# Start of a two-layer decoder: weights of the quantised attention loaded and quantised ahead of the tokens

## The chip, the cores and the metric

One core of one Trainium2 chip. The metric is the device time of one execution in microseconds (us), the median of several runs of the whole program. The profile is one further execution taken by the hardware profiler.

## The reference, cut to what matters

The kernel computes two decoder layers on x of shape (32, 56, 256), float32, with a context of shape (32, 1500, 64). Each layer adds three parts to x in turn, each fed with a layer norm of x:

```python
x = x + quantised_attention(layernorm(x))          # layer 0, the stage of this case
x = x + latent_cross_attention(layernorm(x), ctx)
x = x + mixture_of_experts_16(layernorm(x))
x = x + rotary_attention(layernorm(x))             # layer 1
x = x + causal_cross_attention(layernorm(x), ctx)
x = x + mixture_of_experts_7(layernorm(x))
```

The quantised attention rounds its four weight matrices (256 x 256 each) to -1, 0 or 1 times a scale, the mean magnitude of the whole matrix:

```python
def act_quant(x):
    scale = 127.0 / clip(max(abs(x), axis=-1), EPS)
    return clip(round(x * scale), -128, 127) / scale
def bit_linear(x, W):
    s = clip(mean(abs(W)), EPS)
    return x @ (clip(round(W / s), -1, 1) * s).T
```

The rounding of the weights needs no token; the statistics of the layer norm need no weight. Both must be there before the first tile of tokens can be projected.

## The kernel before, in words

The tokens live in one tile `x_res`, 128 partitions x 16 tiles x 256 values. Two sequences of 56 tokens share a tile of 128 partitions: one on partitions 0 to 55, the other on 64 to 119. Partitions 56 to 63 and 120 to 127 hold no token and must hold zeros.

The program is a row of blocks. In a block every engine has its own list of instructions, and all engines meet at a block's end. The first three blocks are those of this case:

- **Setup** (`setup`, lines 115 to 162). SyncE (SP) loads the identity and a head mask (L143, L144). GpSimd (POOL) writes zeros over all of `x_res` (L153) and then over a tile `zero` (L154). SP waits for the first of these, issues the two loads of the tokens (L148), and waits until all has landed (L149). VectorE (DVE) writes zeros over the eight banks (L158) and converts the identity (L161).
- **Statistics** (`row_stats`, lines 189 to 259). SP loads the quantised stage's weights, 1 MB, with one transfer (L996). Beside this DVE makes the layer norm's statistics: 16 instructions over the 16 tiles of tokens in a loop (L223), 16 that combine them (L228), a copy and an addition (L230, L231), then ScalarE's (ACT) root (L254) and DVE's reciprocal (L234). POOL writes zeros to buffers of the next block. Every later stage calls `row_stats` too.
- **The quantised attention's own block** (`self_attention`, from line 1041). SP waits for the weights, prefetches the six weight tensors of the latent stage (L1939), and then issues three long transfers of zeros to scratch memory that the experts' stages will use (`clear_scratch`, L170, L173). DVE makes a small mask (L1415), then quantises the weights (L1426 to L1459): it sums magnitudes (L1429, L1432), TensorE (PE) adds them over the partitions with one product (L1254), DVE makes scales (L1436, L1438), and each of four matrices is scaled and rounded (L1441, L1442, L1446 or L1450). Then come the 16 tiles of tokens, software-pipelined over all engines; the first instruction of the first tile is the normalisation (L1616).

The order within an engine is the order of the text, written out by hand; a semaphore's wait stops everything behind it on its engine. All the transfers named here are issued by SP and go through its one hardware queue.

Of the kernel before, what the change touches and what calls it, by code (L numbers as in the profile page):

```python
# [7 lines left out]
ALU = mybir.AluOpType  # L8
# [5 lines left out]
AX_X = mybir.AxisListType.X  # L14

P = 128
B, T, D = 32, 56, 256
# [30 lines left out]
def ds(start, size):  # L48
    return bass.ds(start, size)
# [65 lines left out]
def setup(nc, ctx, t):  # L115

    k = {"sems": [], "used": [], "held": ExitStack(), "past": ExitStack()}

    def sb(name, shape, dt=F32):
        return ctx.enter_context(nc.sbuf_tensor(name, shape, dt))  # L120

    k["x"] = sb("x_res", [P, NT, D])
    k["id32"] = sb("id32", [P, P])
    k["id16"] = sb("id16", [P, P], F16)
    k["hmask"] = sb("hmask", [P, 8])
    k["ps"] = ctx.enter_context(nc.psum_tensor("banks", [P, 8, 512], F32))
    k["xg"] = [nc.dram_tensor(f"sent_rows_{layer}", (block_count(layer) * BN + 512, ROW), F16,
                              kind="Internal").ap() for layer in range(2)]
    k["ytok"] = nc.dram_tensor("sent_outputs", (2 * NT * P + block_count(0) * BN, D), F32,
                               kind="Internal").ap()  # L130
    k["zero"] = sb("zero", [P, ROW])
    k["rows_sent"] = [ctx.enter_context(nc.semaphore(f"rows_sent_{c}")) for c in range(2)]
    k["y_sent"] = [ctx.enter_context(nc.semaphore(f"y_sent_{s}")) for s in range(3)]
    k["zeroed"], k["nzero"] = ctx.enter_context(nc.semaphore("scratch_zeroed")), 48
    loaded = ctx.enter_context(nc.semaphore("setup_loaded"))
    loaded_id = ctx.enter_context(nc.semaphore("setup_identity_loaded"))
    zeroed = ctx.enter_context(nc.semaphore("setup_zeroed"))
    x, id32, id16 = k["x"], k["id32"], k["id16"]
    src = t["x"].rearrange("(t two) q d -> two q t d", two=2)
    with nc.Block() as block:  # L140
        @block.sync
        def _(sp):
            sp.dma_start(id32[:], t["ident"]).then_inc(loaded_id, 16)  # L143
            sp.dma_start(k["hmask"][:], t["hmask"]).then_inc(loaded, 16)  # L144

            sp.wait_ge(zeroed, 1)
            for two in range(2):
                sp.dma_start(x[two * HALF:two * HALF + T, :, :], src[two]).then_inc(loaded, 16)  # L148
            sp.wait_ge(loaded, 48)  # L149

        @block.gpsimd
        def _(pool):
            nc.gpsimd.memset(x[:], 0.0).then_inc(zeroed, 1)  # L153
            nc.gpsimd.memset(k["zero"][:], 0.0).then_inc(zeroed, 1)  # L154

        @block.vector
        def _(dve):
            nc.vector.memset(k["ps"][:], 0.0)  # L158

            dve.wait_ge(loaded_id, 16)  # L160
            nc.vector.tensor_copy(id16[:], id32[:])  # L161
    return k


# [21 lines left out]
            sp.wait_ge(stored, 32)  # L186


def row_stats(nc, ctx, name, k, double=False, load=None, zero=None):

# [10 lines left out]
    var_made = new_sem(nc, k, f"{name}_var_made")  # L203
    rooted = new_sem(nc, k, f"{name}_rooted")
    x = k["x"]
    with nc.Block() as block:
        if load:
            block.sync(load)

        @block.gpsimd  # L210
        def _(pool):
# [4 lines left out]
        @block.vector  # L216
        def _(dve):
            s = Steps(dve, own)

            with dve.Fori(0, NT // 8) as n:  # L220
                for u in range(8):
                    i = n * 8 + u
                    nc.vector.bn_stats(  # L223
                        raw[:, ds(i, 1), :].rearrange("p o d -> p (o d)"),
                        x[:, ds(i, 1), :].rearrange("p o d -> p (o d)")).then_inc(own_bn, 1)
            dve.wait_ge(own_bn, NT)
            for i in range(NT):
                s(nc.vector.bn_aggr(mv[:, i, :], raw[:, i, :]))  # L228
            s.settle()
            s(nc.vector.tensor_copy(st["mean"][:], mv[:, :, 0]))  # L230
            nc.vector.tensor_scalar(var[:], mv[:, :, 1], HEPS, None, ALU.add).then_inc(var_made, 1)  # L231

            dve.wait_ge(rooted, 1)
            s(nc.vector.reciprocal(st["r"][:], sd[:, 0, :]))  # L234
            if double:
                s.settle()
                s(nc.vector.tensor_tensor(var[:], mv[:, :, 1], st["r"][:], ALU.mult))
                s.settle()
                s(nc.vector.tensor_tensor(sd[:, 2, :], var[:], st["r"][:], ALU.mult))
                s.settle()  # L240
                s(nc.vector.tensor_scalar(var[:], sd[:, 2, :], HEPS, None, ALU.add))
                s.settle()
                nc.vector.tensor_scalar(sd[:, 0, :], sd[:, 2, :], float(D) / 4, None,
                                        ALU.mult).then_inc(var_made, 1)

                dve.wait_ge(rooted, 3)
                s(nc.vector.reciprocal(sd[:, 2, :], sd[:, 1, :]))
                s.settle()
                s(nc.vector.tensor_tensor(st["rt"][:], st["r"][:], sd[:, 2, :], ALU.mult))
# [637 lines left out]
def self_attention(nc, k, t, kind, prefetch=None):  # L887
# [9 lines left out]
    with ExitStack() as ctx:  # L897
# [3 lines left out]
        def sem(name):  # L901
            return new_sem(nc, k, f"{kind}_{name}")
# [50 lines left out]
        if bit:  # L953
# [8 lines left out]
            ones, one = sb("ones", [P, P]), sb("one", [P, 1])  # L962
            E2, magic = sb("E2", [P, H, T]), sb("magic", [P, 2])
            wsum_done, asum_made, vq_made = sem("weight_sums_done"), sem("asum_made"), sem("vq_made")
            yo_made, x_added, e2_made = sem("outputs_made"), sem("outputs_added"), sem("scaled_exp_made")
        elif rot:
            NW = 768
# [68 lines left out]
                nc.gpsimd.memset(magic[:, 0:1], MAGIC).then_inc(own_pool, 1)  # L1036
                nc.gpsimd.memset(magic[:, 1:2], -MAGIC).then_inc(own_pool, 1)

        st = row_stats(nc, ctx, f"{kind}_stats", k, double=rot, load=load_weights, zero=zero_buffers)

        with nc.Block() as block:
            @block.sync
# [203 lines left out]
            def _(pe):  # L1246
# [1 line left out]
                pe.wait_ge(loaded, NLOAD)  # L1248
                rounds = 2 if bit else 4
                hp = H // rounds  # L1250
                if bit:

                    pe.wait_ge(asum_made, 1)
                    nc.tensor.matmul(Y[:, 0:4], ones[:], asum[:], start=True,  # L1254
                                     stop=True).then_inc(wsum_done, 1)
                if not rot:
                    pe.wait_ge(dve_prepared, 1)

# [147 lines left out]
            def _(dve):  # L1406
                s = Steps(dve, own)

                def then(ins):

                    s(ins)
                    s.settle()
# [9 lines left out]
                        hgm[:], m4[:].unsqueeze(2).broadcast_to([P, 4, 2]),  # L1422
                        hgb[:].unsqueeze(1).broadcast_to([P, 4, 2]), ALU.mult))
                dve.sem_inc(m4_made, 1)
                if bit:
                    s(nc.vector.memset(ones[:], 1.0))  # L1426
                    for m in range(4):
                        for c in range(2):
                            s(nc.vector.tensor_reduce(dq[:, 2 * m + c:2 * m + c + 1], wraw[:, c, m, :],  # L1429
                                                      AX_X, ALU.add, apply_absolute_value=True))  # L1430
                    s.settle()
                    nc.vector.tensor_reduce(asum[:], dq[:, 0:8].rearrange("p (m c) -> p m c", c=2),  # L1432
                                            AX_X, ALU.add).then_inc(asum_made, 1)

                    dve.wait_ge(wsum_done, 1)
                    then(nc.vector.tensor_scalar(sw[:], Y[:, 0:4], 1.0 / (D * D), QEPS, ALU.mult,  # L1436
                                                 ALU.max))
                    then(nc.vector.reciprocal(rsw[:], sw[:]))  # L1438
                    for m in range(4):
                        wm = wraw[:, :, m, :]  # L1440
                        then(nc.vector.tensor_scalar(wm, wm, rsw[:, m:m + 1], MAGIC, ALU.mult, ALU.add))  # L1441
                        then(nc.vector.tensor_scalar(wm, wm, MAGIC, 1.0, ALU.subtract, ALU.min))  # L1442
                        dst = wq[:, :, m * D:(m + 1) * D] if m < 3 else wo[:]
                        if m < 2:
                            for c in range(2):
                                then(nc.vector.tensor_scalar(  # L1446
                                    dst[:, c].rearrange("p (q a e) -> p q a e", a=2, q=2),
                                    in_halves(wm[:, c]), -1.0, None, ALU.max))
                        else:
                            then(nc.vector.tensor_scalar(dst, wm, -1.0, None, ALU.max))  # L1450
                        if m < 3:
                            then(nc.vector.tensor_copy(
                                swrow[:, 16 * m:16 * m + 16], sw[:, m:m + 1].broadcast_to([P, 16])))
                if causal:
                    then(nc.vector.tensor_copy(idb[:], id32[:]))
                    nc.vector.tensor_copy(cmask[:], cmask32[:].unsqueeze(1).broadcast_to([P, 8, T])
                                          ).then_inc(dve_prepared, 1)
                if bit:
                    nc.vector.tensor_copy(ax[:, 1:2], sw[:, 3:4]).then_inc(dve_prepared, 1)  # L1459
                if not rot:  # L1460
                    dve.wait_ge(dve_prepared, 1)
                dve.wait_ge(prepared, 2)
# [1829 lines left out]
```

## Time and profile before

| | us |
|---|---|
| median of 3 runs | 2020.77 |
| lowest, highest | 2019.04, 2022.14 |
| the profiled execution's own time | 2014.04 |
| its span, first to last instruction | 2012.3 |
| VectorE busy over the span | 1466.8 (73%) |
| TensorE busy over the span | 1526.3 (76%) |

In a line of the timeline the first number is the start in us from the start of the span, the second the busy time; then engine, source line, operation, what it writes and reads, and in brackets the idle time ahead of it with what ended it. `SPq` is SP issuing a transfer: the time there is that of the issue, not of the transfer. `PEq L140` as releaser is the meeting of all engines at a block's end.

### The profile page before, as it was taken

How to read it: one execution, taken by the hardware profiler on the slowest of the kernel's cores; microseconds unless marked ns; L12 is line 12 of the kernel's file. 1: busy time of each engine (PE TensorE's matmuls, PEld its weight loads, DVE VectorE, ACT ScalarE, POOL GpSimd, SP SyncE). 2: the span in 40 equal slices, each digit the busy share in tenths (PEclk: the TensorE clock that was granted, in tenths of full speed). 3: DMA queues.
4: the chain of work that ended last, by engine and by line, in shares of the span. 5: the costliest groups of instructions: out<-in, count | busy, mean ns of one | idle time of the engine just before them, and what ended most of it. 6: DMA issues, size and time to landing. Idle time of an engine off the chain costs nothing. (4 is left out here: it accounts for less than half of the span.)

```text
span 2012.3 us, 37357 instructions
## 1 busy us (share of the span) xinstructions
PE 1526.3 (76%) x12412; PEld 927.7 (46%) x12412; DVE 1466.8 (73%) x2589; ACT 1010.4 (50%) x1630; POOL 643.5 (32%) x636
## 2 busy tenths in 40 slices
PE   0555558799999999999996755953777659956992
PEld 0333336443333333333333745942556436644792
DVE  6989872479999999999996784445766635576674
ACT  0555451376666666666663243532544535544461
POOL 1111100124545454554530144642343200026241
PEclk9756555599999999999997857976788879967996
DMA  7910000011111111111110124551000010023334
GB/s 205 301 40 0 0 0 16 16 26 46 39 48 36 50 34 50 34 50 39 45 26 2 30 87 141 174 165 30 1 1 0 0 24 1 0 78 118 92 110 146
DMA packets 78562, 115.88 MB, mean 58 GB/s; under 512 B 12369, under 2 KB 59401, under 8 KB 78051
## 3 DMA queue, kind: packets, MB, share of 16 engines
q1 hardware_dynamic: 70691, 93.35, 16.8%
q0 software_dynamic: 7776, 21.28, 3.0%
q8 instruction: 58, 0.95, 0.2%
q14 instruction: 37, 0.30, 0.1%
HBM read 59.73 MB, written 40.19 MB: 50 GB/s over the span
## 5 line engine op out<-in xcount | busy, mean ns | idle before, releaser
L2408 DVE TENSOR_TENSOR lat_dsum<-lat_dsum,lat_Pb 125x896 f32<-125x896 f32 x320 | 416.7, 1302 | 58.6 <-ACT lat_Pb L2342 52.1
L2342 ACT ACTIVATE lat_Pb<-banks 125x896 f32<-125x896 f32 x384 | 331.5, 915 | 173.2 <-PE banks L2265 171.9
L2220 PE MATMUL banks<-lat_Pb,lat_kv 125*64 125x448 f32 x1536 | 331.0, 552 | 0.0
L2259 PE MATMUL banks<-lat_QH,lat_kT 128*125 128x448 f16 x768 | 183.7, 361 | 2.9 <-DVE lat_QT L2366 1.9
L2175 POOL TENSOR_TENSOR lat_kk<-lat_rot,lat_kk 125x768 f16<-125x768 f32 x32 | 71.2, 2225 | 315.4 <-ACT lat_kk L2314 315.4
L2220 PEld LDWEIGHTS banks<-lat_Pb,lat_kv 125*64 125x64 f32 x1536 | 93.1, 136 | 153.3 <-issue 152.6
L2259 PEld LDWEIGHTS banks<-lat_QH,lat_kT 128*125 128x125 f16 x768 | 89.4, 136 | 114.1 <-ACT lat_Pb L2342 89.9
L2707 POOL DMA_INDIRECT sent_outputs<-moe_yb,moe_yidx x98 | 94.9, 968 | 120.0 <-ACT moe_yb L2948 104.8
L2843 PE MATMUL banks<-moe_w2d,moe_gT 88*128 (+3 forms) x780 | 103.1, 283 | 17.6 <-DVE moe_gT L3127 14.0
L2265 PE MATMUL banks<-lat_QL,lat_kT 64*125 64x448 f16 x768 | 113.7, 375 | 0.0
L2161 POOL TENSOR_TENSOR lat_rot<-lat_raw,lat_cosK 125x768 f32<-125x768 f32 x32 | 73.7, 2303 | 92.7 <-DMA lat_raw<-in_ctx_dram 88.1
L2381 DVE RECIPROCAL lat_rD<-banks 128x448 f32<-128x448 f32 x32 | 94.3, 2946 | 1.9 <-PE banks L2231 1.9
L2843 PEld LDWEIGHTS banks<-moe_w2d,moe_gT 88*128 88x128 f16 (+1 forms) x780 | 76.4, 101 | 33.2 <-issue 22.6
L2699 POOL DMA_INDIRECT sent_rows<-moe_arena,moe_idx x64 | 72.5, 1133 | 50.5 <-DVE moe_idx L3065 31.4
L3115 DVE COPY moe_xTb<-banks 128x1024 f16<-128x1024 f16 x49 | 33.9, 691 | 65.4 <-PE banks L2810 65.4
L2761 PE MATMUL banks<-moe_xTb,moe_w2i 128*88 128x256 f16 (+1 forms) x588 | 73.4, 275 | 0.0
L2305 ACT ACTIVATE lat_kT<-banks 128x1000 f16<-128x1000 f16 x64 | 51.1, 798 | 31.9 <-PE banks L2207 31.8
L2265 PEld LDWEIGHTS banks<-lat_QL,lat_kT 64*125 64x125 f16 x768 | 36.6, 131 | 63.6 <-issue 63.6
L2761 PEld LDWEIGHTS banks<-moe_xTb,moe_w2i 128*88 (+1 forms) x588 | 62.6, 112 | 4.2 <-issue 1.0
L1123 POOL TENSOR_TENSOR x_res<-x_res,bit_yo 128x256 f32 (+1 forms) x16 | 11.6, 727 | 162.1 <-DVE bit_yo L1495 162.1
L2169 POOL TENSOR_TENSOR lat_rot<-lat_rot 125x768 f32<-125x768 f32 x32 | 58.7, 1834 | 2.5
L427 POOL TENSOR_TENSOR rot_rt<-rot_y,rot_msin 128x256 f32<-128x256 f32 x32 | 34.4, 1074 | 68.8 <-DVE rot_msin L777 67.5
(421 smaller groups left out, 3331.1 us busy)
## 6 DMA issues: line engine op xcount, KB each, us to landing
moe_xb<-sent_rows SPq DMA_DIRECT2D x49, 257.0 KB, 2.9
lat_raw<-in_ctx_dram SPq DMA_DIRECT2D x32, 375.0 KB
moe_arena<-sent_outputs SPq DMA_DIRECT2D x16, 512.0 KB, 7.6
sent_rows<-zero SPq DMA_DIRECT2D x1, 7453.0 KB, 51.3
lat_QH<-lat_QT SPq DMA_DIRECT2D x64, 112.0 KB, 2.2
lat_QL<-lat_QT SPq DMA_DIRECT2D x64, 112.0 KB, 2.2
sent_rows<-zero SPq DMA_DIRECT2D x1, 5140.0 KB, 68.5
sent_outputs<-zero SPq DMA_DIRECT2D x1, 4096.0 KB, 40.9
```

The source lines that it names most:

```text
L2161: s(nc.gpsimd.tensor_tensor(rot[:, par], r, cosK[:], ALU.mult))
L2175: nc.gpsimd.tensor_tensor(halves(par, True), paired(rot[:, par]), halves(par, False), ALU.subtract).then_inc(kl_made, 1)
L2220: ins = nc.tensor.matmul(ps[u * DC:(u + 1) * DC, 4 + par, 0:8 * T], kv[:, par, tt, :], Pb[:, tt % NPB, u, :], start=tt == 0, stop=tt == KT ...
L2259: nc.tensor.matmul(ps[0:KP, 2 * u + tt % 2, 0:8 * T], kT[:, par, tt, 0:KP], queries(QH, u), start=True, stop=False)
L2265: ins = nc.tensor.matmul(ps[0:KP, 2 * u + tt % 2, 0:8 * T], kT[rows, par, tt, 0:KP], queries(QL, u, rows), start=False, stop=True)
L2342: nc.scalar.activation(Pb[:, slot:slot + 2, u, :], ps[0:KP, 2 * u:2 * u + 2, 0:8 * T], ACT.Exp, scale=1.0 / QSCALE).then_inc(exp_done, 1)
L2381: s(nc.vector.reciprocal(rD[:], ps[:, 7, 0:8 * T]))
L2408: ins = nc.vector.tensor_tensor(dsum[:, par], dsum[:, par], Pb[:, tt % NPB], ALU.add)
L2699: nc.gpsimd.indirect_dma_start(xg[:, :], bass.IndirectOffsetOnAxis(ap=idx[:, c, i:i + 1], axis=0), rows[:, i, :], None).then_inc((sent0, s ...
L2707: nc.gpsimd.indirect_dma_start(ytok[:, :], bass.IndirectOffsetOnAxis(ap=yidx[:, n, h:h + 1], axis=0), yb[:, n % 3, h, :], None).then_inc(y ...
L2761: ins = nc.tensor.matmul(ps[0:FP, dst, j * BN:(j + 1) * BN], w[:, u, c, j * FP:(j + 1) * FP], rhs(v, c), start=a + c == 0, stop=a == 2 and ...
L2843: ins = nc.tensor.matmul(dst, gT2[:, n % 2, u, j, h * P:(h + 1) * P], w[:, v, j, :], start=a + j == 0, stop=last and not (gated and b < 0))
```

## The change

- Setup keeps the identity, the mask and the `zero` tile. The writing of zeros over `x_res` and the loads of the tokens leave it.
- The loads of the tokens become a function `load_x`, issued by SP in the statistics block behind the load of the weights. The tokens come in two parts of eight tiles. Each part has four transfers: two for the token rows and two that copy zeros from the `zero` tile to the eight unused partitions of each half. Each part has a semaphore of its own.
- DVE's quantisation of the weights, word for word as it was, and PE's product for the sums move from the attention's block to the head of the statistics block. DVE then waits for the first part of the tokens, makes eight statistics, waits for the second part and makes eight more. In this call the loop over the tiles is written out.
- In the attention's block the small mask (L1415) stays where it is.

```diff
@@ setup
+    x_in = [ctx.enter_context(nc.semaphore(f"x_loaded_{part}")) for part in range(2)]
...
-            sp.wait_ge(zeroed, 1)
-            for two in range(2):
-                sp.dma_start(x[two * HALF:two * HALF + T, :, :], src[two]).then_inc(loaded, 16)
-            sp.wait_ge(loaded, 48)
+            sp.wait_ge(loaded, 16)
...
-            nc.gpsimd.memset(x[:], 0.0).then_inc(zeroed, 1)
             nc.gpsimd.memset(k["zero"][:], 0.0).then_inc(zeroed, 1)
...
+    def load_x(sp):
+        sp.wait_ge(zeroed, 1)
+        for part in range(2):
+            tiles = slice(part * NT // 2, (part + 1) * NT // 2)
+            for two in range(2):
+                r = two * HALF
+                sp.dma_start(x[r:r + T, tiles, :], src[two, :, tiles, :]).then_inc(x_in[part], 16)
+                sp.dma_start(x[r + T:r + HALF, tiles, :], k["zero"][0:HALF - T, 0:D].unsqueeze(1)
+                             .broadcast_to([HALF - T, NT // 2, D])).then_inc(x_in[part], 16)
+
+    k["load_x"], k["x_in"] = load_x, x_in
@@ row_stats
+    load_x = k.pop("load_x", None)
     with nc.Block() as block:
-        if load:
-            block.sync(load)
+        @block.sync
+        def _(sp):
+            if load:
+                load(sp)
+            if load_x:
+                load_x(sp)
+
+        if sums:
+            block.tensor(sums)
...
         @block.vector
         def _(dve):
             s = Steps(dve, own)
-
-            with dve.Fori(0, NT // 8) as n:
+            if ready:
+                ready(dve)
+
+            def eight(n):
                 for u in range(8):
...
+            if load_x:
+                for part in range(2):
+                    dve.wait_ge(k["x_in"][part], 64)
+                    eight(part)
+            else:
+                with dve.Fori(0, NT // 8) as n:
+                    eight(n)
@@ self_attention
+            own_weights = sem("dve_weights")
...
+        def quantised_weights(dve):
+            s = Steps(dve, own_weights)
...
+            dve.wait_ge(loaded, NLOAD)
+            s(nc.vector.memset(ones[:], 1.0))
...
+            nc.vector.tensor_copy(ax[:, 1:2], sw[:, 3:4]).then_inc(dve_prepared, 1)
+
+        def weight_sums(pe):
+            pe.wait_ge(asum_made, 1)
+            nc.tensor.matmul(Y[:, 0:4], ones[:], asum[:], start=True, stop=True).then_inc(wsum_done, 1)
+
+        st = row_stats(nc, ctx, f"{kind}_stats", k, double=rot, load=load_weights, zero=zero_buffers,
+                       ready=quantised_weights if bit else None, sums=weight_sums if bit else None)
...
-                if bit:
-
-                    pe.wait_ge(asum_made, 1)
-                    nc.tensor.matmul(Y[:, 0:4], ones[:], asum[:], start=True,
-                                     stop=True).then_inc(wsum_done, 1)
...
-                if bit:
-                    s(nc.vector.memset(ones[:], 1.0))
...
-                if bit:
-                    nc.vector.tensor_copy(ax[:, 1:2], sw[:, 3:4]).then_inc(dve_prepared, 1)
```

The lines left out in the last part are the body of the quantisation, the same in the old place and the new.

## Rows read from the trace of the kernel before

**Rows 1.** Timeline, VectorE alone, from the start to the first normalisation.

```profile
1.75 3.47 DVE L158 MEMSET banks<- 128x4096 f32 x1 [1.75 <-PEq L3282]
5.13 0.21 DVE L161 CAST id<-id 128x128 f16<-128x128 f32 x1
17.53 5.32 DVE L223 BATCH_NORM_STATS2 bit_stats_raw<-x_res  x16 [12.19 <-PEq L140]
...
24.62 0.25 DVE L234 RECIPROCAL bit_stats_r<-bit_stats_sd 128x16 f32<-128x16 f32 x1 [0.28 <-ACT bit_stats_sd L254]
25.20 0.16 DVE L1415 TENSOR_TENSOR bit_m<-hmask 128x4 f32<-128x4 f32 x1 [0.33 <-PEq L206]
25.57 0.17 DVE L1426 MEMSET bit_ones<- 128x128 f32 x1 [0.20 <-DVE bit_m L1415]
...
36.44 0.15 DVE L1459 COPY bit_ax<-bit_sw 128x1 f32<-128x1 f32 x1
36.63 0.41 DVE L1616 TENSOR_SCALAR bit_xtmp<-x_res,bit_stats_mean,bit_stats_r 128x256 f32<-128x256 f32 x1
```

**Rows 2.** Timeline, SyncE's issues, to the last transfer of zeros.

```profile
0.81 0.43 SPq L143 DMA_DIRECT2D id<-in_ident_dram  x1
1.30 0.41 SPq L144 DMA_DIRECT2D hmask<-in_hmask_dram  x1
4.35 0.92 SPq L148 DMA_DIRECT2D x_res<-in_x_dram  x2
17.18 0.41 SPq L996 DMA_DIRECT2D bit_wraw<-in_bit_w_dram  x1
25.14 0.56 SPq L1939 DMA_DIRECT2D lat_wqr<-in_lat_wqr_dram  x1
...
28.45 38.14 SPq L170 DMA_DIRECT2D sent_rows<-zero  x2
66.64 18.43 SPq L173 DMA_DIRECT2D sent_outputs<-zero  x1
```

**Rows 3.** Waits of SyncE: who waited for whom, total us, times, longest us.

```profile
SPq L140 <- DMA x_res<-in_x_dram: 11.5, 1, 11.5
```

**Rows 4.** Windows at the start: us, busy by engine, granted clock, DMA share, GB/s.

```profile
4.00:6.00 2.00, 0.00 (x0) 0.00 (x0) 1.34 (x2) 0.00 (x0) 0.79 (x2) 1.00 0.13 36
...
14.00:16.00 2.00, 0.00 (x0) 0.00 (x0) 0.00 (x0) 0.00 (x0) 0.00 (x0) 1.00 0.72 123
...
18.00:19.00 1.00, 0.00 (x0) 0.00 (x0) 1.00 (x4) 0.47 (x1) 1.00 (x2) 1.00 0.73 78
...
21.00:22.00 1.00, 0.00 (x0) 0.00 (x0) 1.00 (x4) 0.00 (x0) 0.00 (x0) 1.00 0.49 197
```

**Rows 5.** Transfers issued before 70 us: KB each, us from issue to landing.

```profile
sent_outputs<-zero SPq DMA_DIRECT2D x1, 4096.0 KB, 40.9
lat_wq<-in_lat_wq_dram SPq DMA_DIRECT2D x1, 2048.0 KB, 18.2
...
x_res<-in_x_dram SPq DMA_DIRECT2D x2, 896.0 KB
...
bit_wraw<-in_bit_w_dram SPq DMA_DIRECT2D x1, 1024.0 KB, 4.9
lat_wqr<-in_lat_wqr_dram SPq DMA_DIRECT2D x1, 768.0 KB, 6.4
...
id<-in_ident_dram SPq DMA_DIRECT2D x1, 64.0 KB, 1.9
```

**Rows 6.** Windows over three tiles each of the quantised stage, columns as in rows 4.

```profile
59.86:109.40 49.54, 27.38 (x212) 17.68 (x216) 44.30 (x116) 27.12 (x43) 5.32 (x8) 0.69 0.98 288
109.40:158.50 49.10, 27.20 (x191) 16.78 (x184) 44.43 (x116) 24.20 (x39) 6.03 (x9) 0.53 0.00 0
```

**Rows 7.** First users of what SyncE sends ahead: timeline of TensorE, tile `sent_rows`.

```profile
314.13 1.51 PE L1983 MATMUL banks<-lat_wkr,lat_wqr 64*96 64x64 f32 x8 [3.53 <-PEq L1041]
...
L2699 POOL DMA_INDIRECT sent_rows<-moe_arena,moe_idx x64: 956/962/5527, 1187.9 to 1867.3; - x64
```

More of the change, by code:

```diff
@@ L186, in _, with row_stats @@
             sp.wait_ge(stored, 32)
-def row_stats(nc, ctx, name, k, double=False, load=None, zero=None):
+def row_stats(nc, ctx, name, k, double=False, load=None, zero=None, ready=None, sums=None):
     def sb(n, shape):
@@ L1037, in zero_buffers, with then @@
                 nc.gpsimd.memset(magic[:, 1:2], -MAGIC).then_inc(own_pool, 1)
-        st = row_stats(nc, ctx, f"{kind}_stats", k, double=rot, load=load_weights, zero=zero_buffers)
+        def quantised_weights(dve):
+            s = Steps(dve, own_weights)
+            def then(ins):
+                s(ins)
+                s.settle()
+            dve.wait_ge(loaded, NLOAD)
+            s(nc.vector.memset(ones[:], 1.0))
+            for m in range(4):
+                for c in range(2):
+                    s(nc.vector.tensor_reduce(dq[:, 2 * m + c:2 * m + c + 1], wraw[:, c, m, :],
+                                              AX_X, ALU.add, apply_absolute_value=True))
+            s.settle()
+            nc.vector.tensor_reduce(asum[:], dq[:, 0:8].rearrange("p (m c) -> p m c", c=2),
+                                    AX_X, ALU.add).then_inc(asum_made, 1)
+            dve.wait_ge(wsum_done, 1)
+            then(nc.vector.tensor_scalar(sw[:], Y[:, 0:4], 1.0 / (D * D), QEPS, ALU.mult,
+                                         ALU.max))
+            then(nc.vector.reciprocal(rsw[:], sw[:]))
+            for m in range(4):
+                wm = wraw[:, :, m, :]
+                then(nc.vector.tensor_scalar(wm, wm, rsw[:, m:m + 1], MAGIC, ALU.mult, ALU.add))
+                then(nc.vector.tensor_scalar(wm, wm, MAGIC, 1.0, ALU.subtract, ALU.min))
+                dst = wq[:, :, m * D:(m + 1) * D] if m < 3 else wo[:]
+                if m < 2:
+                    for c in range(2):
+                        then(nc.vector.tensor_scalar(
+                            dst[:, c].rearrange("p (q a e) -> p q a e", a=2, q=2),
+                            in_halves(wm[:, c]), -1.0, None, ALU.max))
+                else:
+                    then(nc.vector.tensor_scalar(dst, wm, -1.0, None, ALU.max))
+                if m < 3:
+                    then(nc.vector.tensor_copy(
+                        swrow[:, 16 * m:16 * m + 16], sw[:, m:m + 1].broadcast_to([P, 16])))
+            nc.vector.tensor_copy(ax[:, 1:2], sw[:, 3:4]).then_inc(dve_prepared, 1)
@@ L1424, in _ @@
                 dve.sem_inc(m4_made, 1)
-                if bit:
-                    s(nc.vector.memset(ones[:], 1.0))
[L1427 to L1453, printed above, removed]
                 if causal:
```

## The prediction

> **What bounds the kernel now.** The change touches only the first 37 us of 2012, so I read that stretch and not the average shares. First VectorE's timeline [rows 1]: it finishes the setup at 5.34 (5.13 plus 0.21), stands idle for 12.19 us, makes statistics from 17.53, and from 25.57 to 36.59 (36.44 plus 0.15) quantises weights. At 36.63 the first tile of tokens is normalised. Between 17.53 and 36.63 VectorE hardly stops. So the start is one chain: tokens land, statistics, weights, first tile. Then SyncE's issues and waits [rows 2, 3]: the tokens are issued at 4.35 and SyncE waits 11.5 us for them, which is what VectorE's idle time is made of. The weights are issued only at 17.18, since the block of the tokens must end first; they are on the way while VectorE makes statistics. The last thing to see is that the two inputs differ in what they cost. The weights, 1024 KB, land 4.9 us after their issue [rows 5]. The tokens, 2 x 896 KB, keep the DMA busy from about 5.7 (it is busy for 0.13 of the window 4 to 6) to about 15.4 (0.72 of the window 14 to 16), and SyncE sees the end at about 16.8 [rows 3, 4]. The quick transfer is started last, behind the slow one. After the start VectorE is what the 16 tiles go by: it is busy for 44.3 of 49.5 us over three of them [rows 6].
>
> **The setup block** loses SyncE's long wait. What is left on each engine: VectorE until 5.34 [rows 1]; SyncE the identity, landed 1.9 us after its issue at 0.81, and the head mask, issued at 1.30 and far smaller [rows 2, 5]. No row gives the mask's landing; by the identity's it is at 3.2, so VectorE covers it. The zeros over the token tile are gone from GpSimd, but they too lay beside VectorE's work, so their removal by itself is worth nothing: they only held the tokens' issue, until 4.35. A block's end costs about 0.27 us: VectorE's last result before the next one is at 24.87, SyncE's next issue at 25.14 [rows 1, 2]. So the weights are issued at 5.34 + 0.27 = 5.61 in place of 17.18.
>
> **The weights land** at 5.61 + 4.9 = 10.5. That is their own row, with nothing queued behind them. Now eight transfers are queued behind. The first of the latent stage's loads, 768 KB with five more behind, took 6.4 [rows 5]; that gives 12.0 as the late end. Below 4.9 there is nothing to expect. I take 4.9, the same transfer, and keep the 1.5 us for the range.
>
> **VectorE's chain** is then: quantisation 36.59 - 25.57 = 11.0 us, PE's product and its wait included, giving 21.6. The statistics from their first instruction to the next block's first, 25.20 - 17.53 = 7.67 us, giving 29.25. The small mask with its wait, 25.57 - 25.20 = 0.37. The first normalisation starts at 29.6 against 36.63: **7.0 us less**. All of it is the 17.53 - 10.5 by which the chain starts sooner. No instruction of VectorE goes away, so the gain is idle time alone. The written-out loop and the waits are equal to the row within 0.3 us either way (VectorE starts 0.35 us after SyncE behind the meeting at 17.18, part of it the loop's set-up) [rows 1, 2]. TensorE and ScalarE have nothing else in that block; GpSimd's fills, 3 us, lie beside the wait for the weights.
>
> **Are the tokens there in time?** They are needed at 21.6 (first part) and, after eight statistics of 5.32 / 16 us each, at 24.3 (second part). SyncE issues nine transfers from 5.61, at about 0.45 each done by 9.8 [rows 2]: not a limit. In the queue's order the tokens follow the weights, whose bytes stopped moving at about 21.5 with an issue at 17.18 (0.49 of the window 21 to 22) [rows 2, 4]. In the new time base that is 10.0. The tokens' bytes take 15.4 - 5.7 = 9.7 us, so to 19.7, and the receipt 16.8 - 15.4 = 1.4 more: 21.1. The first part is there by about 17, well before 21.6. To this come four transfers of zeros, 256 KB in pieces of 1 KB, which the profile of before doesn't show. At the least they cost nothing (they may fill in where the tokens leave DMA engines unused). Priced as tokens, byte for byte, they add 9.7 x 256 / 1792 = 1.4 us: 22.5, under 24.3. At the most, if what counts is the number of partitions written (8 a transfer against 56 at equal bytes for each partition), each takes as long as a token transfer of its part, 9.7 / 4, and the four add 9.7: 30.8, that is 6.5 us late. The pieces, the queue and the source row are nearest to the tokens' own row, so I take 1.4, and **the tokens cost nothing**, with 1.8 us to spare. If that cover goes, each us of lateness beyond 24.3 is paid in full by VectorE.
>
> The Trainium skill speaks against this slack ("SBUF — State Buffer", Door 1: The DMA port swizzle): bandwidth depends on how many of 16 ports the partitions reach, and eight adjacent partitions 56 to 63 reach two. With its 435 GB/s over 16 ports a transfer of 64 KB would take about 1.2 us, an estimate from that page. Four of them would then add 4.8 us in place of 1.4 and the second part would land at 25.9, 1.6 us late; the gain would be 5.4. The trace of before has no transfer to eight partitions, so it shows neither.
>
> **What is moved past what.** The prefetch of the latent weights and the zeros to scratch memory start when the statistics block ends, at about 29.2 in place of 25.14: 4 us later. Their first users are at 314 and 1188 [rows 7], and the last of these transfers, behind the latent loads in the queue, landed at 66.64 + 40.9 = 107.5 [rows 2, 5]; at 112 it still has some 195 us to spare before the first user. I cost this at nothing. They now run 11 us later relative to the tiles of tokens, but three tiles under full DMA load took 49.54 us and three without any 49.10 [rows 6], so shifting that load is worth under 0.1 us. VectorE has no other wait added.
>
> **Sum**: -7.0 from the chain, 0 from the tokens, 0 elsewhere. Against the profiled execution's own 2014.04 (1.7 above its span of 2012.3) this is 2007.0. The profiled run is 6.7 below the median of the runs, more than the gain itself; I apply the difference to the median: 2020.8 - 7.0 = **2013.8**. A measurement of this kernel tells about 0.2%, 4.0 us, from no change. The three runs lie 3.1 us apart.
>
> **Rivals.**
> 1. **The second part is somewhat late**, by 1 to 3 us. Its cover is 24.3 - 21.1 = 3.2, so the four transfers of zeros must add 4.2 to 6.2, 1.1 to 1.6 each; the bounds above are 0.35 and 2.4 each. Then 4.0 to 6.0 remain, 2014.8 to 2016.8. Weights that land at 12.0 give the same: 5.5. For it: no row prices a transfer to eight partitions, and this lies midway between the bounds. Against it: the byte-for-byte price leaves 1.8 us. 20%. (The port estimate above, 1.2 us each, falls at its near end.)
> 2. **The zeros are as slow as whole token transfers**: the second part lands at 30.8, then eight statistics (2.66) and the rest of the chain up to the mask's end, 25.57 - 22.85 = 2.7: normalisation at 36.2. The gain is 0.4, 2020.4, no change. The wait has only gone from one end of the chain to the other. 7%.
> 3. **The weights are held up by the tokens** in the same queue, so that both land together at 22.5. Then VectorE's chain of 19.1 us starts there: 22.5 + 19.1 = 41.6, slower by 5.0, 2025.8. It decides at the wait ahead of the quantisation, and the tie is a landing at 17.5. Against it: the latent loads landed in the order of issue, 6.4 for the first and 18.2 for a later one [rows 5]. 4%.
> 4. **The chain shortens but the time doesn't follow**: 7 us are gained at the start and given back by a later stage that meets other clock or DMA phases. Nothing in the stage waits for a fixed time, so I see no place for it; yet the run-to-run spread is near half of the gain. Result within 4 us of before. 9%, a third of it on the slow side by chance.
> 5. **The change doesn't do what it says**: the two parts would be needless, since VectorE comes to the tokens only at 21.6. That changes the use of the split and not the sum, and has no share of its own.
>
> **How the numbers follow.** My forecast has 60%, the rivals 20, 7, 4 and 9. Faster by over 0.2%: 57 of the 60 (the rest to noise), 16 of the 20, 2 of the others: 0.75. Slower: 4 and 2, 0.06. Same: the remaining 0.19. The range: below, 7.3 us plus 2.5 of drift gives 2011. Above, it takes in the first rival and most of the noise: 2018.8.
>
> **What would show it.** VectorE's timeline of after should have: the first sum of magnitudes at 10.6, the first statistic at 21.6 with no wait, the ninth at 24.3 with no wait, the first normalisation at 29.6. The wait ahead of the quantisation should name the weights' transfer, landing 4.9 after an issue at 5.6. From the first normalisation on, all tiles should lie 7.0 us sooner, and the first product of the latent stage at 307 in place of 314. An idle time ahead of the ninth statistic proves the first or second rival, by its length; one ahead of the first sum beyond 10.6 the third. The prediction is wrong if the first normalisation is later than about 32.6.

## The result, and the profile after

The change makes the kernel faster by a third of a per cent: median 2012.56 us (17 runs) against 2019.04 us (17 runs of the kernel before), ratio 0.9965 with a 95% interval of 0.9951 to 0.9978. That is 7.1 us less by the ratio (2019.04 x 0.0035), 4.4 to 9.9 us by its interval, and 6.5 us by the medians. The forecast was 2013.8 us, 7.0 us less. The kernel before was measured anew beside the change, and its median over 17 runs lies 1.7 us under the 2020.77 on which the forecast was built.

VectorE's timeline of the kernel after, from the start to the first normalisation, answers to [rows 1]:

```profile
1.75 3.47 DVE L155 MEMSET banks<- 128x4096 f32 x1 [1.75 <-PEq L3318]
5.13 0.21 DVE L158 CAST id<-id 128x128 f16<-128x128 f32 x1
10.84 0.17 DVE L1076 MEMSET bit_ones<- 128x128 f32 x1 [5.50 <-DMA bit_wraw<-in_bit_w_dram]
10.92 2.64 DVE L1079 TENSOR_REDUCE bit_dq<-bit_wraw 128x1 f32<-128x256 f32 x8
...
21.64 0.15 DVE L1104 COPY bit_ax<-bit_sw 128x1 f32<-128x1 f32 x1
21.71 5.31 DVE L242 BATCH_NORM_STATS2 bit_stats_raw<-x_res 128x6 f32<-128x256 f32 x16
27.06 1.17 DVE L255 BATCH_NORM_AGGREGATE bit_stats_mv<-bit_stats_raw 128x2 f32<-128x6 f32 x16
...
29.37 0.16 DVE L1482 TENSOR_TENSOR bit_m<-hmask 128x4 f32<-128x4 f32 x1 [0.33 <-PEq L216]
29.76 0.41 DVE L1652 TENSOR_SCALAR bit_xtmp<-x_res,bit_stats_mean,bit_stats_r 128x256 f32<-128x256 f32 x1 [0.23 <-DVE bit_m L1482]
```

The idle time ahead of VectorE's first real work has shrunk from 12.19 us to 5.50, and what ends it is now the weights' transfer and no longer the end of the block with the tokens. Behind it the 16 statistics stand in one piece: 5.31 us without a gap, so neither wait for the tokens cost anything. The first normalisation starts at 29.76 in place of 36.63, 6.87 us sooner.

SyncE's issues in the kernel after answer to [rows 2]; the transfers' table gives size and time to landing, as in [rows 5]:

```profile
5.61 0.39 SPq L1024 DMA_DIRECT2D bit_wraw<-in_bit_w_dram  x1
6.04 0.50 SPq L166 DMA_DIRECT2D x_res<-in_x_dram  x1
6.59 0.89 SPq L167 DMA_DIRECT2D x_res<-zero  x1
...
10.37 0.53 SPq L166 DMA_DIRECT2D x_res<-in_x_dram  x1
10.94 2.10 SPq L167 DMA_DIRECT2D x_res<-zero  x1
29.32 0.57 SPq L1975 DMA_DIRECT2D lat_wqr<-in_lat_wqr_dram  x1
```

```profile
bit_wraw<-in_bit_w_dram SPq DMA_DIRECT2D x1, 1024.0 KB, 5.2
...
x_res<-zero SPq DMA_DIRECT2D x4, 64.0 KB
```

The weights are issued at 5.61 and land in 5.2 us. SyncE's nine issues last until 13.04 (10.94 plus 2.10), and not until 9.8 as forecast: those of the zeros take 0.71 to 2.10 us each. It costs nothing, since the DMA is never without work meanwhile: its share is 0.88 or more in every microsecond from 8 to 20. The 6.9 us arrive at the next stage undiminished; the timeline of TensorE, as in [rows 7]:

```profile
307.18 1.51 PE L2019 MATMUL banks<-lat_wkr,lat_wqr 64*96 64x64 f32 x8 [3.53 <-PEq L1113]
```

That is 6.95 us ahead of the 314.13 of before. At the end of the span the two profiles lie 5.7 us apart (2006.6 against 2012.3). Between, each stage adds or takes some tenths; the last section takes this scatter up.

### The profile page after: what moved, and what is told of

Its sections match the earlier page's. It is cut to its first block and busy times, and to the rows that moved or that the text cites. A ratio compares the mean times of both kernels' runs of the same rounds, so it can differ in the third digit from the quotient of the medians.

```text
span 2006.6 us, 37326 instructions
## 1 busy us (share of the span) xinstructions
PE 1526.6 (76%) x12412; PEld 928.0 (46%) x12412; DVE 1466.8 (73%) x2589; ACT 1010.3 (50%) x1630; POOL 642.7 (32%) x635
```

## The experiments

Each kernel is the kernel after with the edit shown, if nothing else is said. Each ratio is to runs of the kernel before taken beside it. "First normalisation" is the start of the first instruction of the first tile: 36.63 before, 29.76 after.

**The loads moved alone.** VectorE keeps the order of before.

```diff
             s = Steps(dve, own)
-            if ready:
-                ready(dve)
...
             s(nc.vector.reciprocal(st["r"][:], sd[:, 0, :]))
+            if ready:
+                ready(dve)
```

> The loads moved alone: weights and tokens issued in the statistics block as in the change, but VectorE makes the statistics first and quantises after them, as before. My theory: the gain needs the order as well. The second part of the tokens lands at about 21.9 (DMA quiet at 20.8 in the profile of the change, plus 1.1), then 2.7 for eight statistics and 13.8 for the rest of the chain: first normalisation at 38.3, so 1.7 us later than before and 8.5 later than the change. Rival (the earlier loads alone bring the gain): first normalisation at 30 to 32.

Ratio to before 1.0015 (1.0004 to 1.0027, 10 runs): 3.0 us slower. Its timeline of VectorE, with the waits now in the open:

```profile
17.80 2.71 DVE L239 BATCH_NORM_STATS2 bit_stats_raw<-x_res 128x6 f32<-128x256 f32 x8 [12.46 <-DMA x_res<-zero]
22.97 2.71 DVE L239 BATCH_NORM_STATS2 bit_stats_raw<-x_res 128x6 f32<-128x256 f32 x8 [2.46 <-DMA x_res<-zero]
...
39.35 0.41 DVE L1651 TENSOR_SCALAR bit_xtmp<-x_res,bit_stats_mean,bit_stats_r 128x256 f32<-128x256 f32 x1 [0.23 <-DVE bit_m L1481]
```

The first normalisation is at 39.35, 2.7 us later than before. I had expected 38.3; work on the second part began 1.1 later than the 21.9 assumed. Loading early gains nothing while the work that needs the slow input stands first: VectorE is idle for 12.46 + 2.46 us, with weights on hand from about 10.9.

**The order moved alone.** The tokens are loaded in the setup block, as before; VectorE quantises first.

```diff
-            sp.wait_ge(loaded, 16)
+            sp.wait_ge(zeroed, 1)
+            for two in range(2):
+                sp.dma_start(x[two * HALF:two * HALF + T, :, :], src[two]).then_inc(loaded, 16)
+            sp.wait_ge(loaded, 48)
...
+            nc.gpsimd.memset(x[:], 0.0).then_inc(zeroed, 1)
...
-    k["load_x"], k["x_in"] = load_x, x_in
```

> The order moved alone: VectorE quantises first, but the tokens are loaded in the setup block and the weights only behind it, as before. My theory: VectorE stands idle for the weights, 22.1 + 11.0 + 7.67 + 0.37: first normalisation at 41.2, 4.6 us later than before, total about 4.6 us above before. Rival (the order alone is worth something): at or before 36.6.

Ratio 1.0016 (1.0006 to 1.0025, 10 runs), 3.2 us slower. VectorE's timeline:

```profile
22.77 0.17 DVE L1079 MEMSET bit_ones<- 128x128 f32 x1 [17.43 <-DMA bit_wraw<-in_bit_w_dram]
...
41.97 0.41 DVE L1655 TENSOR_SCALAR bit_xtmp<-x_res,bit_stats_mean,bit_stats_r 128x256 f32<-128x256 f32 x1 [0.23 <-DVE bit_m L1485]
```

One idle time of 17.43 us, and the first normalisation 5.3 us later than before. Of these 0.64 are the tokens, which landed later in this execution (the weights were issued at 17.82 and not 17.18); the rest, 4.7 us, is what was expected (4.6). The timed runs show less than that, 3.2 us with an upper end of 5.0; a difference of this size is at the limit of what the runs resolve. So neither half of the change is worth anything by itself. By the timed runs each alone costs 3 us; together they gain 7.

**The order in the queue.** The tokens' eight transfers are issued ahead of the weights.

```diff
-            if load:
-                load(sp)
             if load_x:
                 load_x(sp)
+            if load:
+                load(sp)
```

> The change with the weights issued behind the tokens' eight transfers. My theory, a queue served in the order of issue: the weights land last, at 22 to 23, quantisation starts then, first normalisation at 41 to 42; total 4 to 5 us above before and 11 to 12 above the change. Rival (the engines share the transfers out evenly whatever the order, which is the third rival of the prediction): the weights would land at about the same time as in the change within 2 us and the order of issue would not matter.

Ratio 1.0027 (1.0015 to 1.0040, 10 runs): 5.4 us slower than before. VectorE's timeline and the weights' landing:

```profile
23.14 0.17 DVE L1076 MEMSET bit_ones<- 128x128 f32 x1 [17.80 <-DMA bit_wraw<-in_bit_w_dram]
...
42.05 0.41 DVE L1652 TENSOR_SCALAR bit_xtmp<-x_res,bit_stats_mean,bit_stats_r 128x256 f32<-128x256 f32 x1 [0.23 <-DVE bit_m L1482]
```

```profile
bit_wraw<-in_bit_w_dram SPq DMA_DIRECT2D x1, 1024.0 KB, 11.9
```

and SyncE's issue of the weights:

```profile
11.17 0.46 SPq L1024 DMA_DIRECT2D bit_wraw<-in_bit_w_dram  x1
```

The same instructions with two lines exchanged are 12.3 us later at the first normalisation. The weights land at 23.1 in place of 10.8, a little over the 22 to 23 expected. Two things add up to this: SyncE needs until 11.17 to issue the eight transfers ahead, which makes the weights' issue 5.6 us later, and then they take 11.9 us to land in place of 5.2, 6.7 us more. The rival written down here, a landing within 2 us of the change's, falls.

This run by itself doesn't tell a queue served in the order of issue from one whose work is shared out evenly: what is issued last would land last in either. The kernel after does. There the tokens' first transfer is issued 0.43 us behind the weights, and the weights land in 5.2 us against 4.9 with nothing behind them. The DMA's share and GB/s at the end of these rows show it too, first two windows of the kernel after and then one of the kernel before, when the weights moved alone:

```profile
8.00:9.00 1.00, 0.00 (x0) 0.00 (x0) 0.00 (x0) 0.00 (x0) 0.41 (x4) 1.00 1.04 426
...
11.00:12.00 1.00, 0.00 (x0) 0.00 (x0) 1.00 (x5) 0.00 (x0) 0.00 (x0) 1.00 1.00 182
```

```profile
20.00:21.00 1.00, 0.00 (x0) 0.00 (x0) 1.00 (x4) 0.00 (x0) 0.00 (x0) 1.00 1.00 414
```

426 GB/s is the rate of the weights alone (414), and only behind them comes the rate at which the tokens moved before (172 to 187 between 8 and 14). So the tokens waited for the weights, and the even sharing of the third rival is ruled out.

**The price of the zeros' transfers.** The loads-only kernel once more, with GpSimd filling the token tile in the setup block and no transfer of zeros; the waits for the two parts are set to match. It was timed once.

```diff
-                sp.dma_start(x[r + T:r + HALF, tiles, :], k["zero"][0:HALF - T, 0:D].unsqueeze(1)
-                             .broadcast_to([HALF - T, NT // 2, D])).then_inc(x_in[part], 16)
...
+            nc.gpsimd.memset(x[:], 0.0).then_inc(zeroed, 1)
             nc.gpsimd.memset(k["zero"][:], 0.0).then_inc(zeroed, 1)
```

> The loads-only kernel (statistics first, quantisation after) with the four transfers of zeros taken out; GpSimd fills the whole token tile with zeros in the setup block instead, as before. Here VectorE waits openly for both parts, so the start of the ninth statistic shows the landing, with and without the zeros' transfers. My theory: the four transfers cost no more than byte for byte, so the ninth statistic starts 0.5 to 1.5 us sooner than in the loads-only kernel. Rival (two ports of sixteen, 1.2 us each): about 4.8 us sooner. Second rival (as slow as token transfers): 9.7 sooner.

```profile
15.75 2.71 DVE L238 BATCH_NORM_STATS2 bit_stats_raw<-x_res 128x6 f32<-128x256 f32 x8 [10.40 <-DMA x_res<-in_x_dram]
20.62 2.71 DVE L238 BATCH_NORM_STATS2 bit_stats_raw<-x_res 128x6 f32<-128x256 f32 x8 [2.16 <-DMA x_res<-in_x_dram]
```

The second part is there at 20.62 in place of 22.97: the four transfers of zeros cost 2.35 us. That is over the 0.5 to 1.5 that I expected and under both rivals. Most of it (17.80 - 15.75 = 2.05) already shows in the first part, with two of the four; why the last two add so little was not taken apart. The windows tell where the end of it lies, first with the zeros' transfers, then without (share and GB/s at the end):

```profile
20.00:21.00 1.00, 0.00 (x0) 0.00 (x0) 0.51 (x2) 0.00 (x0) 0.00 (x0) 1.00 0.55 168
```

```profile
20.00:21.00 1.00, 0.00 (x0) 0.00 (x0) 0.38 (x2) 0.00 (x0) 0.00 (x0) 1.00 0.00 0
```

Without them the DMA is quiet from 20 on. With them it goes on to about 21.5, on average with only half of its 16 engines busy (0.55). So the zeros' price is in part a tail in which the work is spread unevenly; which engines carry it, no view here shows. By the Trainium skill ("SBUF — State Buffer", Door 1: The DMA port swizzle) the estimate was 4.8 us, if the four overlapped neither with each other nor with the tokens. The measured 2.35 is half of that, so here the estimate from the page's figure was a bound from above; that it is the ports that set the 2.35, no run shows.

**One part in place of two**, and **GpSimd's fill in place of the transfers of zeros**, both in the kernel after. The edit of the first is shown; the second has the edit of the experiment above.

```diff
-                    dve.wait_ge(k["x_in"][part], 64)
+                    if part == 0:
+                        dve.wait_ge(k["x_in"][0], 64)
+                        dve.wait_ge(k["x_in"][1], 64)
```

> The change with one wait for both parts ahead of the first statistic. My theory: the second part lands just as VectorE is done with the weights, at 21.9 against 21.7, so the split is worth 0.2 to 0.5 us. Rival (the split carries the gain): first statistic 2 us or more later than 21.7.

> The change with GpSimd's fill of the whole token tile in the setup block in place of the four transfers of zeros. My theory: both lie under other work, the fill ends by 4.8 and VectorE holds the setup until 5.34, so the first normalisation stays at 29.8 within 0.2 us. Rival (writing the zeros by transfer is part of the gain): 30.5 or later.

VectorE's timeline with one wait, and then the first normalisation with GpSimd's fill:

```profile
22.38 5.33 DVE L242 BATCH_NORM_STATS2 bit_stats_raw<-x_res 128x6 f32<-128x256 f32 x16 [0.67 <-DMA x_res<-zero]
```

```profile
29.80 0.41 DVE L1651 TENSOR_SCALAR bit_xtmp<-x_res,bit_stats_mean,bit_stats_r 128x256 f32<-128x256 f32 x1 [0.22 <-DVE bit_m L1481]
```

The split into two parts saves one idle time of 0.67 us, more than the 0.2 to 0.5 expected; the whole landing at 22.4 is only just behind VectorE, which is free at 21.7. With GpSimd's fill the start is the same within 0.04 us (29.80 against 29.76). The parts of the change are thus worth: loads and order together all but 0.7 us, the two parts 0.7, the transfer of zeros nothing. The last two belong together: without the zeros' transfers the second part was there at 20.62 in the loads-only kernel, before VectorE is free at 21.7. So with GpSimd's fill the tokens should need no split at all; that kernel was not run. Each of the two kernels of this experiment was timed once (2014.76 and 2014.33 us, against 2020.88 for the kernel before), and the verdict rests on the rows.

**Without a setup block.** If the weights' landing sets the start, issuing them still sooner must pay further. Here everything of the setup moves into the statistics block: the weights are the first transfer of all, VectorE clears the banks while they arrive, and the identity is converted during the wait for the root.

```diff
-    with nc.Block() as block:
-        @block.sync
...
+    cleared = ctx.enter_context(nc.semaphore("setup_banks_cleared"))
+    def clear_banks(dve):
+        nc.vector.memset(k["ps"][:], 0.0).then_inc(cleared, 1)
...
             if load:
                 load(sp)
+            if first:
+                first["small"](sp)
             if load_x:
                 load_x(sp)
+            if first:
+                first["waited"](sp)
...
             s = Steps(dve, own)
+            if first:
+                first["banks"](dve)
...
+            if first:
+                first["id16"](dve)
             dve.wait_ge(rooted, 1)
```

> The change without a setup block of its own: weights issued at the very start, then identity, mask, tokens; VectorE clears the banks while the weights arrive and converts the identity while it waits for the root. My theory: the weights' landing sets the start, issue at 0.8 in place of 5.6, landing at 6.0, first normalisation at 25.0, 4.8 us sooner than in the change; the tokens' first part lands by 13, the second by 17.5, needed at 17.1 and 19.7. Total 11.5 us below before (ratio about 0.994). Rival (the tokens' transfers now bound the statistics): idle time ahead of the first or ninth statistic and less than 4 us gained over the change.

Ratio to before 0.9963 (0.9950 to 0.9977, 6 runs). Its timeline of VectorE:

```profile
5.89 0.17 DVE L1090 MEMSET bit_ones<- 128x128 f32 x1 [0.67 <-DMA bit_wraw<-in_bit_w_dram]
...
16.82 5.31 DVE L254 BATCH_NORM_STATS2 bit_stats_raw<-x_res 128x6 f32<-128x256 f32 x16
...
24.88 0.41 DVE L1666 TENSOR_SCALAR bit_xtmp<-x_res,bit_stats_mean,bit_stats_r 128x256 f32<-128x256 f32 x1 [0.23 <-DVE bit_m L1496]
```

The start does what was expected: first normalisation at 24.88, 4.9 us ahead of the change, with no wait for the tokens. But the total was only 7.5 us below before by the ratio, where 11.5 was expected. This asked for a repeat, on one chip with the change and the kernel before.

> The change itself once more, on the same chip as the next run, to see how far one profile of the same program differs from another in the stages behind the start. First normalisation at 29.8 and first product of the latent stage at 307.2, both within 0.2; the stages behind these may lie up to 3 us apart from the first profile. Total 6 to 7 us below before.

> The kernel without a setup block once more, beside the change on one chip. Theory one (its 4.9 us at the start reach the end, and the first measurement of it was low by scatter): 11 to 12 us below before, about 5 below the change. Theory two (a later stage takes back some 3 us of it every time): the gap between the two kernels shrinks at the same stage as in the first profile, between 1129 and 1606 us, and the total stays at 7 to 9 below before.

> The kernel before once more, for the scatter of its later stages. First normalisation at 36.6 to 37.3 (the tokens' landing scatters by about half a us), the experts' first statistics 1104 us behind it; the total within 0.3% of the first profile. If the stages behind the start differ by 2 us or more from its first profile, differences of that size between kernels there mean nothing.

These three ran on another chip, where the kernel before takes 2053.46 us (13 runs). The change had a ratio of 0.9962 (0.9949 to 0.9976, 8 runs), 7.8 us less; the kernel without a setup block 0.9948 (0.9934 to 0.9962, 7 runs), 10.7 us less. The first normalisations were at 30.01, 24.96 and 37.00, and the first product of the latent stage in the change at 307.27, as expected. The scatter behind them was not: the change's first experts' stage took 243.8 us in place of 220.1, where I had allowed 3 us in all, and the kernel before took 2052.58 us in its profiled run, 1.9% and not 0.3% over its first. So a length of a late stage is to be compared within one chip. The columns below are duration min/median/max in ns, and first and last start in us, for the statistics that open the later stages, first in the kernel without a setup block in its first profile, then in its second:

```profile
L254 DVE BATCH_NORM_STATS2 moe_stats_raw<-x_res x32: 407/409/428, 1129.0 to 1776.3; - x32
...
L254 DVE BATCH_NORM_STATS2 rot_stats_raw<-x_res x16: 407/409/428, 1349.2 to 1354.1; - x16
...
L254 DVE BATCH_NORM_STATS2 causal_stats_raw<-x_res x16: 407/409/429, 1606.4 to 1611.6; - x16
```

```profile
L254 DVE BATCH_NORM_STATS2 moe_stats_raw<-x_res x32: 407/409/427, 1129.3 to 1793.5; - x32
...
L254 DVE BATCH_NORM_STATS2 rot_stats_raw<-x_res x16: 407/409/427, 1372.2 to 1377.1; - x16
...
L254 DVE BATCH_NORM_STATS2 causal_stats_raw<-x_res x16: 407/409/427, 1624.0 to 1629.1; - x16
```

Up to the experts the two agree within 0.3 us, and the gain over before is whole: 1140.8 - 1129.0 = 11.8. The rotary stage, from its statistics to those of the causal stage, took 257.2 us in the one and 251.8 in the other. On the second chip the change took 253.9 us for it and the kernel before 255.3. So the 3 us that the first profile lost there (254.3 in the profile of before) is not a toll that this kernel pays each time: in the repeat it was the quickest of the three. The second theory falls, by this one repeat. The first holds as far as the runs resolve it: 10.7 us is just short of the 11 to 12 that it asked for, and only 2.9 below the change where it asked for 5. The intervals of the change and of this kernel still overlap, in the first measurements of the two as on this chip, and that it beats the change is shown by the start of the traces, by 4.9 us, and only made likely by the times.

## Why the prediction was right

- **The setup block ends at 5.34 and the weights are issued at 5.61**: 5.61, to the hundredth. The mask landed 1.7 us after its issue, well under cover.
- **The weights land at 10.5**: 5.2 us after the issue and not 4.9, work begins at 10.84. Transfers queued behind cost 0.3 us, not the 1.5 of the bound (the prediction writes the end of the quantisation as 21.6, where 10.5 + 11.0 is 21.5; nothing hangs on it). The exchange of the two loads shows that this term carries the whole result: 12.3 us hang on the order of two lines. The third rival falls: with the tokens queued right behind, the weights landed at 10.8 and not at 22.5.
- **VectorE's chain**: quantisation forecast as 11.0 us, measured 21.79 - 10.84 = 10.95; from the first statistic to the mask 7.67, measured 29.37 - 21.71 = 7.66. First normalisation forecast at 29.6, measured at 29.76.
- **The tokens are in time**: second part forecast at 22.5, measured at 22.4 and 22.97 in the two kernels that wait for it openly, needed at 24.4. In the kernel after itself the landing is hidden behind the quantisation; it shows only that it was in time. The term of the zeros was sized at 1.4 us and measured at 2.35; the tokens and their receipt came a little sooner than I had them (20.6 against 21.1), which made up for half of it. The first rival needed 4.2 us there and had its mechanism right, but not its size; the second needed 9.7 and falls.
- **Nothing lost behind it**: first product of the latent stage forecast at 307, measured at 307.18. The prefetch and the zeros to scratch memory start at 29.3, forecast 29.2, and no wait for them appeared. The fourth rival, a result within 4 us of before, falls narrowly by the timed runs, whose interval begins at 4.4.
- **The sum**: 7.0 us forecast, 7.1 by the ratio. That these agree to a tenth is luck, since the interval is 4.4 to 9.9; the start of the trace, 6.87 us, is the firmer witness. That the absolute 2013.8 lies 1.2 from the measured 2012.56 is mostly the kernel before, which the three runs had put 1.7 too high. What went wrong on the way: SyncE's nine issues were taken as 0.45 us each, done by 9.8, and lasted until 13.04. Also, I took the split into two parts as needless, though it is worth 0.67 us. By my own number of 22.5 against 21.6 for VectorE it had to be worth 0.9; the fifth rival drew the wrong conclusion from a right sum.

## What to carry to other kernels

Where one engine needs two inputs and one is quick to load and long to prepare, and the other slow to load and quick to use, issue the quick one first and work on it while the slow one arrives. Change the order of the issues and the order of the work together: each alone made this kernel 3 us slower, because the wait only moved. Then look for what still stands ahead of the first issue: here a block of small chores held it for another 4.9 us at the start of the trace, a gain that the timed runs make likely but do not resolve.

## What the runs showed of the hardware

- A transfer's place in its queue was worth more than its size. The same 1024 KB landed 4.9 us after the issue with nothing behind (three profiles), 5.0 to 5.4 us with four to ten transfers behind, and 11.9 us with eight ahead, which also made its issue 5.6 us later.
- Zeros copied to 8 partitions by four transfers of 64 KB held up the tokens by 2.35 us (one profile with them, one without): 256 KB, a seventh of the tokens' bytes, for about a quarter of the 9.7 us that all the tokens' bytes take.
- Stages far behind the change differ from profile to profile, and from one chip to the next. The first experts' stage, up to the rotary stage's statistics, took 219.6 to 220.9 us in nine profiles and 240.9 to 243.8 in the three of the last chip, whatever the kernel (whether the chip makes this difference or the time at which it was used, these runs don't tell); the rotary stage 251.8 to 257.3 over all twelve. The stretch up to the experts held within 2.2 us (1104.1 to 1106.3 from the first normalisation on). A gain of 7 us can be read to a tenth at the start of the trace, while it takes some 17 timed runs to see it in the whole at plus or minus 3 us.
